# A message-passing layer over a 5000 x 5000 matrix: where each column group's first loads land, when the neighbour counts are spread, and x in two pieces

## The chip, the cores and the metric

The kernel runs on one core of one Trainium2 chip. The metric is the device time of one execution in microseconds (us), lower is better. The kernel before was timed three times: median 266.12 us, from 265.71 to 266.26.

## The reference

`x` is 5000 x 64, `adj` is 5000 x 5000, all in 32-bit floats:

```
h = maximum(layernorm(x), 0)
neighbors = (adj @ h) / (num_neighbors[:, None] + 1e-7)
out = x + relu(concatenate([h, neighbors]) @ fc_w.T + fc_b)
```

Nearly all the data is the matrix: 100 MB of it are read once. `fc_w` is 64 x 128, so its left half works on `h` itself and its right half on the sum over the neighbours.

## The kernel before

The right half of `fc_w` is applied to `h` before the large product (`weigh` on TensorE, copied to `g_sb` by `copy_g` on ScalarE), so that the large product gives the weighted neighbour sums at once. The matrix is handed over transposed, its rows (the inner dimension, 5000) cut into 39 **tiles** of 128 and a rest of 8 rows. Nine blocks of four tiles and one of three make ten **steps** m = 0 to 9.

**Column groups.** The columns (the nodes of the output) are cut into three groups, each stored for itself: group 0 has 2048 columns, group 1 has 2560, group 2 the last 392. TensorE goes through all 39 tiles for group 0, then for group 1, then for group 2. `multiply` (line 544) multiplies one tile for all columns of the group. It issues 8 MATMUL records a tile in group 0, 12 in group 1 and 4 in group 2 (a 32-bit product takes two). The sums stay in the PSUM tiles `acc` (for group 2 it is the tile that is named `turned`). `remainder` (line 555) adds the rest of 8 rows once per group, from `adj_rem`.

**Loads.** SyncE (SP) issues the loads of the matrix one after another into one buffer `raw` of 32768 elements a lane, all on one queue. `STEPS` gives how many tiles one load of each step has, 4, 2 or 1. The loads are numbered through: 0 to 9 are group 0, 10 to 22 group 1, 23 to 36 group 2. A load of four tiles has 4.19 MB in group 0, 5.24 MB in group 1 and 0.80 MB in group 2. `place(n)` says where in `raw` a load lands. Each group uses the buffer as a ring of so many tiles from a start: `RING` holds the start and the length, both in tiles of that group. Group 0 has a ring of 16 tiles from element 0, group 1 of 12 tiles (30720 elements) from element 0, group 2 of 60 tiles from its tile 20 (element 7840).

**What lets a load start.** The last MATMUL of a load counts `load_used` up. `loads_before(n)` finds the last earlier load whose place overlaps that of load n, and SP waits for `load_used` to pass it before it issues load n. SP issues in order, so a load behind a waiting one waits too. TensorE waits for each load's own semaphore before its first tile.

```
return max([k + 1 for k in range(n) if place(k) < place_end(n) and place(n) < place_end(k)] + [n - LANDINGS + 1, 0])
```

**Other work on TensorE.** Tables that are keyed by (group, tile) say after which tile something else is done: `TURN_AFTER` and `WEIGH_AFTER` (transposing `h` and weighing it, set by set, in group 0), `SPREAD_AFTER` (five `spread` calls, lines 523 to 533), `REM_AFTER` (`remainder`) and `FLIP_AFTER` (turning the finished sums back, lines 569 to 571). `spread(b)` turns the reciprocals of the neighbour counts into the layout of the sums; ScalarE copies each result to `rnn_bc` (`copy_spread`, line 309), and `spread(b)` from the third on waits for the copy of the one two before. VectorE multiplies the finished sums with them (`scale`, line 422, behind `wait_sums`) and, after the flip, adds and clips (`finish`).

**The start.** SP first loads `x` (1.18 MB, line 226) and its last nodes, then the matrix. ScalarE issues the weights `w_both` and the bias on its own queue. VectorE and ScalarE normalize `x` in five sets. TensorE can transpose the first set, but waits for `w_both` before it weighs it, and group 0's tile 0 needs that result.

Of the kernel before, what the change touches and what calls it, by code (L numbers as in the profile page):

```python
# [13 lines left out]
BLOCK = 512  # L14
RUN = BLOCK // LANES
# [14 lines left out]
GROUPS = [(0, 4, 0), (4, 5, 2), (9, 1, 5)]  # L30
ALIGN = 1


STEPS = [(4, 4, 4, 4, 4, 4, 4, 4, 4, 4), (4, 4, 4, 4, 4, 4, 4, 4, 2, 1), (4, 4, 4, 4, 4, 4, 4, 2, 2, 1)]
RING = [(0, 16), (0, 12), (20, 60)]


def gnn_layer(nc, x, adj_groups, num_neighbors, fc_t, fc_b, out):
# [23 lines left out]
    BT = 2 * RUN  # L62
    SETS = TILES // BT
    PAIRS = FULL // 2
    ALONE, LAST = PAIRS, PAIRS + 1
    WIDTH = [v.shape[1] for v in adj_groups]
    WIDEST = max(WIDTH) // BLOCK

# [2 lines left out]

    def sides(g, b):

        w = BLOCK if b < ALONE else BLOCK // 2 if b == ALONE else SIDE
        c = (b - GROUPS[g][2]) * 2 * BLOCK
        return [(0, c, w), (1, c + w, w)]


# [7 lines left out]
    def place(n):  # L86

        g, m, i0, _ = LOADS[n]
        return (RING[g][0] + (m * RUN + i0) % RING[g][1]) * WIDTH[g]

    def place_end(n):
        return place(n) + (LOADS[n][3] - LOADS[n][2]) * WIDTH[LOADS[n][0]]

    def loads_before(n):

        return max([k + 1 for k in range(n) if place(k) < place_end(n) and place(n) < place_end(k)] + [n - LANDINGS + 1, 0])

    assert max(place_end(n) for n in range(len(LOADS))) <= RAW


    TURN_AFTER = {(0, 3): 1, (0, 7): 2, (0, 13): 3, (0, 21): 4}
    WEIGH_AFTER = {(0, 5): 1, (0, 11): 2, (0, 19): 3, (0, 27): 4}
    SPREAD_AFTER = {(0, 31 + b): b for b in range(SETS)}
    REM_AFTER = {(0, 37): 0, (1, 11): 1, (2, 3): 2}
    FLIP_AFTER = {(1, 7): 0, (1, 9): 1, (2, 9): 2, (2, 13): 3, (2, 17): 4}
    PRELOAD_AFTER = (2, 25)
    LN_OPS = 8
# [1 line left out]
    with ExitStack() as ctx:  # L109
# [105 lines left out]
        @block.sync  # L215
        def _(sp):
            def load(n):
                g, m, i0, i1 = LOADS[n]
                w = WIDTH[g]
                if loads_before(n):  # L220
                    sp.wait_ge(load_used, loads_before(n))
                r = RUN if m < FULL else TAIL_RUN
                rows = adj_groups[g][m * BLOCK:m * BLOCK + r * LANES, 0:w].rearrange("(p i) c -> p (i c)", i=r)
                sp.dma_start(raw[:, place(n):place_end(n)], rows[:, i0 * w:i1 * w]).then_inc(loaded(n)[0], 16)

            sp.dma_start(flat(x_sb[:, 0:ROWS, :]), x[0:TAIL0, :].rearrange("(p r) f -> p (r f)", r=ROWS)
                         ).then_inc(x_loaded[0], 16)
            sp.wait_ge(x_cleared, 1)
            sp.dma_start(tail(x_sb), tail_nodes(x)).then_inc(x_loaded[1], 16)
            for n in range(len(LOADS)):  # L230
                load(n)
            sp.wait_ge(out_ready, LAST + 1)
            sp.dma_start(tail_nodes(out), tail(out_sb)).then_inc(last_stored, 16)
            sp.wait_ge(last_stored, 16)
# [11 lines left out]
        def _(act):  # L246
# [58 lines left out]

            def copy_spread(b):
                act.wait_ge(spread_done, b + 1)
                w = BLOCK if b < PAIRS else BLOCK // 2 + SIDE
                nc.scalar.activation(rnn_bc[:, b, 0:w], y[b % 2][:, 0:w], ACT.Copy).then_inc(spread_copied, 1)  # L309

            def store(g):
# [29 lines left out]
        def _(dve):  # L341
# [13 lines left out]

            def normalize(b):
                base = LN_OPS * b
                dve.wait_ge(x_loaded[0], 16)
                if b == SETS - 1:
                    dve.wait_ge(x_loaded[1], 16)  # L360
                for rows, narrow, wide in parts(b):
# [50 lines left out]

            def wait_sums(g, b):
                dve.wait_ge(load_used, (FIRST_LOAD + [len(LOADS)])[g + 1])
                dve.wait_ge(spread_copied, min(b, SETS - 1) + 1)

            def scale(g, b):

# [15 lines left out]

            def scale_last(g):
                wait_sums(g, LAST)
                dve.wait_ge(flipped, PAIRS)
                for i in range(2):
                    nc.vector.tensor_tensor(sums[0][:, i * LAST_LANES:(i + 1) * LAST_LANES],
                                            tile_major(acc[LAST][:, 0:SIDE], 2)[:, i, :],  # L440
                                            rnn_bc[:, ALONE, BLOCK // 2 + i * LAST_LANES:BLOCK // 2 + (i + 1) * LAST_LANES],
                                            ALU.mult).then_inc(scaled, 1)

            def finish(b):
                m0, m1 = 2 * b, min(2 * b + 2, FULL)
                o, to_add = blocks(out_sb, m0, m1), blocks(x_sb, m0, m1)
                dve.wait_ge(flipped, b + 1)
                nc.vector.tensor_tensor(o, split(y[b % 2][:, 0:RUN * F * (m1 - m0)]), o, ALU.add).then_inc(summed, 1)  # L448
                dve.wait_ge(summed, b + 1)
                nc.vector.scalar_tensor_tensor(o, o, 0.0, to_add, ALU.max, ALU.add).then_inc(out_ready, 1)  # L450
# [19 lines left out]
            add_bias(3)  # L470
            prepare_halves()
            add_bias(4)
            for b in banks(0):
                scale(0, b)
            for b in banks(0):
                finish(b)
            scale(1, 2)
            scale(1, 3)
            scale_alone(1)
            for b in banks(1):  # L480
                finish(b)
            scale_last(2)
            finish_last()

        @block.tensor
        def _(pe):
# [27 lines left out]
            def spread(b):  # L514
# [2 lines left out]
                    pe.wait_ge(self_copied, 2 * SETS)  # L517
                else:
                    pe.wait_ge(spread_copied, b - 1)
                if b < PAIRS:  # L520
                    for i in range(RUN):
                        t = i * FULL + 2 * b
                        last = nc.tensor.matmul(y[b % 2][:, i * LANES:(i + 1) * LANES], flat(rnn_wide[:, t:t + 2, :]),  # L523
                                                ident[:], start=True, stop=True)
                else:
                    for s in range(2):
                        k = slice(s * HALF, (s + 1) * HALF)
                        for i in range(RUN):
                            last = nc.tensor.matmul(y[b % 2][k, i * HALF:(i + 1) * HALF], rnn_wide[:, i * FULL + FULL - 1, :],  # L529
                                                    ident[:, k], start=True, stop=True, tile_position=(0, s * HALF))  # L530
                        for i in range(2):
                            c = BLOCK // 2 + i * LAST_LANES
                            last = nc.tensor.matmul(y[b % 2][k, c:c + LAST_LANES], rnn_wide[:, ROWS + 2 * s + i, :],
                                                    ident[:, 0:LAST_LANES], start=True, stop=True,
                                                    tile_position=(0, s * HALF))
# [24 lines left out]
            def flip(b):  # L560
# [4 lines left out]
                    pe.wait_ge(out_ready, b - 1)  # L565
                for i in range(RUN):
                    c = slice(i * LANES, (i + 1) * LANES)
                    if b < PAIRS:
                        last = nc.tensor.transpose(y[b % 2][:, c], sums[b % 2][:, c], ident[:])  # L569
                    else:  # L570
                        last = nc.tensor.matmul(y[b % 2][:, i * F:(i + 1) * F], cen[:, c], ident_twice[:],  # L571
# [20 lines left out]
            for n in range(len(LOADS)):  # L592
                g, m, i0, i1 = LOADS[n]
                pe.wait_ge(*loaded(n))
                for i in range(i0, i1):
# [5 lines left out]
                        turn(TURN_AFTER[at])  # L601
                    if at in WEIGH_AFTER:
                        weigh(WEIGH_AFTER[at])
                    if at in SPREAD_AFTER:
                        if SPREAD_AFTER[at] == 0:
                            pe.wait_ge(rnn_chain, 3)
                        spread(SPREAD_AFTER[at])
                    if at in REM_AFTER:
                        remainder(REM_AFTER[at])
                    if at in FLIP_AFTER:  # L610
# [31 lines left out]
```

## Time and profile before

| | us |
|---|---|
| median of three runs | 266.12 |
| lowest and highest | 265.71, 266.26 |
| the profiled execution, own time | 265.64 |
| its span | 263.9 |
| TensorE matmuls busy | 203.5 (77%) |
| VectorE busy | 35.9 |
| ScalarE busy | 15.2 |

The profile is of one execution. Its span runs from the first to the last record; its own time is 1.74 us longer. The queue of SP moved 101.22 of the 102.84 MB; the mean over the span is 390 GB/s. The chain of waits that ended last lies 51% on transfers and 47% on TensorE. In a view of windows, "DMA share" is the mean busy share of the 16 DMA engines; a short window can show over 1, since a transfer's packets are counted where they are recorded. "PEclk" is the clock that TensorE was granted, 1.00 for 2.4 GHz and 0.50 for 1.2 GHz.

### The profile page before, as it was taken

To read this page: it belongs to the slowest core of one execution; us is meant where nothing else is said; L and a number is where in the kernel's file an instruction comes from. 1 tells how busy PE (TensorE), PEld (TensorE's weight loads), DVE (VectorE), ACT (ScalarE), POOL (GpSimd) and SP (SyncE) were. 2 spreads that over 40 slices of the span, in tenths; PEclk is the share of its full clock that TensorE was granted. 3 is DMA by queue.
4 is the path that set the end of the run, shared out by engine and by line. 5 is a ranking of instruction groups with operands and counts; after the bars stand their busy time and mean duration, and the time that the engine had idled before them with its cause. 6 is when DMAs were issued, how large, how long until landed. Compare 5 with 4: busy or idle time off the path is not lost.

```text
span 263.9 us, 2548 instructions
## 1 busy us (share of the span) xinstructions
PE 203.5 (77%) x1156; PEld 89.2 (34%) x1156; DVE 35.9 (14%) x80; ACT 15.2 (6%) x35; POOL 3.0 (1%) x8
## 2 busy tenths in 40 slices
PE   0102899999999979950199959786969859999995
PEld 0102334343334425620033324232323313344784
DVE  0730036333500100010000022000000000000521
ACT  2210011120010001100000000000000000000000
POOL 4000000000000000000000000000000000000000
PEclk9999999999999999995569999997979997999999
DMA  7999999999999994039999999999999999999992
GB/s 279 400 441 385 438 417 441 428 422 446 407 442 427 435 416 205 2 112 422 460 410 447 447 397 456 435 420 410 456 440 428 405 430 419 427 421 421 418 398 79
DMA packets 7848, 102.84 MB, mean 390 GB/s; under 512 B 1478, under 2 KB 3286, under 8 KB 4766
## 3 DMA queue, kind: packets, MB, share of 16 engines
q1 hardware_dynamic: 5892, 101.22, 90.4%
q10 hardware_dynamic: 1946, 1.46, 1.7%
q8 instruction: 9, 0.15, 0.2%
q14 instruction: 1, 0.01, 0.0%
HBM read 101.40 MB, written 1.28 MB: 389 GB/s over the span
## 4 chain that ended last, share of the span: by engine, by line
DMA 51%; PE 47%; ACT 1%; DVE 0%; issue 0%; SPq 0%
DMA raw<-adj_group 42%; PE acc L544 36%; DMA w_both<-fc_t 9%; PE turned L544 5%; PE y L506 2%; PE y L523 1%; PE turned L493 1%; PE acc L555 1%; PE y L569 0%; PE y L571 0%; ACT L318 0%; PE y L529 0%; ACT g_sb L303 0%; PE y L579 0%; DVE out_sb L456 0%
## 5 line engine op out<-in xcount | busy, mean ns | idle before, releaser
L544 PE MATMUL acc<-raw,g_sb 128*64 128x512 f32 (+1 forms) x780 | 166.1, 579 | 33.5 <-DMA raw<-adj_group 32.5
L544 PEld LDWEIGHTS acc<-raw,g_sb 128*64 128x64 f32 x780 | 58.1, 143 | 130.6 <-issue 86.7
L422 DVE TENSOR_TENSOR sums<-acc,rnn_bc 128x512 f32<-128x512 f32 x4 | 2.6, 686 | 109.8 <-PE acc L544 109.8
L506 PE MATMUL y<-w_both,ht 64*128 64x128 f32 (+1 forms) x80 | 7.6, 317 | 12.4 <-DMA w_both<-fc_t 12.4
L544 PE MATMUL turned<-raw,g_sb 128*64 128x196 f32 x156 | 14.2, 332 | 0.0
L493 PE MATMUL turned<-ident,h_pairs 128*128 128x128 f32 x20 | 3.7, 315 | 11.5 <-DVE h_pairs L385 11.5
L506 PEld LDWEIGHTS y<-w_both,ht 64*128 64x128 f32 x80 | 6.2, 215 | 16.1 <-DMA w_both<-fc_t 12.8
L544 PEld LDWEIGHTS turned<-raw,g_sb 128*64 128x64 f32 x156 | 10.8, 137 | 2.2 <-issue 0.3
L448 DVE TENSOR_TENSOR out_sb<-y,out_sb 128x512 f32<-128x512 f32 (+1 forms) x5 | 3.2, 638 | 45.5 <-PE y L569 44.4
L394 DVE TENSOR_TENSOR out_sb<-y,bias 128x256 f32<-128x256 f32 x10 | 3.8, 420 | 39.8 <-ACT g_sb L303 20.7
L493 PEld LDWEIGHTS turned<-ident,h_pairs 128*128 128x128 f32 x20 | 2.4, 156 | 14.7 <-issue 13.1
L303 ACT ACTIVATE g_sb<-y 128x256 f32<-128x256 f32 x10 | 3.3, 381 | 40.2 <-PE y L506 28.3
L523 PEld LDWEIGHTS y<-ident,rnn_wide 128*128 128x128 f32 x32 | 3.9, 191 | 3.2 <-issue 3.2
L523 PE MATMUL y<-ident,rnn_wide 128*128 128x128 f32 x32 | 4.6, 288 | 0.0
L373 DVE TENSOR_REDUCE var<-sums 128x8 f32<-128x512 f32 x5 | 3.4, 686 | 8.6 <-ACT sums L277 8.6
L555 PE MATMUL acc<-adj_rem,g_sb 128*64 128x512 f32 (+1 forms) x20 | 4.5, 549 | 0.0
L362 DVE TENSOR_REDUCE mean<-x_sb 128x8 f32<-128x512 f32 (+1 forms) x6 | 3.5, 590 | 5.1 <-DMA x_sb<-x 5.1
L297 ACT ACTIVATE ht<-turned 128x512 f32<-128x512 f32 x5 | 3.0, 597 | 19.0 <-PE turned L493 19.0
L309 ACT ACTIVATE rnn_bc<-y 128x512 f32<-128x512 f32 (+1 forms) x5 | 2.9, 587 | 19.1 <-PE y L523 16.5
L369 DVE TENSOR_TENSOR cen<-x_sb,mean 128x512 f32<-128x512 f32 (+1 forms) x6 | 3.5, 602 | 0.2
L277 ACT ACTIVATE sums<-cen 128x512 f32<-128x512 f32 x5 | 3.1, 625 | 7.2 <-DVE cen L369 5.9
L381 DVE TENSOR_TENSOR cen<-cen,rstd 128x512 f32<-128x512 f32 x5 | 3.5, 691 | 0.2
(48 smaller groups left out, 38.6 us busy)
## 6 DMA issues: line engine op xcount, KB each, us to landing
raw<-adj_group SPq DMA_DIRECT2D x8, 5120.0 KB, 27.6
raw<-adj_group SPq DMA_DIRECT2D x9, 4096.0 KB, 25.2
raw<-adj_group SPq DMA_DIRECT2D x7, 784.0 KB, 19.5
raw<-adj_group SPq DMA_DIRECT2D x2, 2560.0 KB, 23.3
raw<-adj_group SPq DMA_DIRECT2D x3, 1280.0 KB, 21.5
raw<-adj_group SPq DMA_DIRECT2D x1, 3072.0 KB, 26.8
raw<-adj_group SPq DMA_DIRECT2D x4, 392.0 KB, 20.5
x_sb<-x SPq DMA_DIRECT2D x1, 1152.0 KB, 5.7
```

What stands on the lines that cost most here:

```text
L303: nc.scalar.activation(g_sb[:, t0:t0 + RUN, :], split(y[s][:])[:, :, F:2 * F], ACT.Copy).then_inc(g_copied, 1)
L362: last = nc.vector.tensor_reduce(narrow(mean[:]), rows, AX_X, ALU.add)
L369: last = nc.vector.tensor_tensor(wide(cen[:]), rows, m.unsqueeze(len(m.shape)).to_broadcast(list(rows.shape)), ALU.subtract)
L373: nc.vector.tensor_reduce(var[:], sums[0][:].rearrange("p (t f) -> p t f", f=F), AX_X, ALU.add).then_inc(ln_dve, 1)
L381: nc.vector.tensor_tensor(c, c, bcast(rstd[:]), ALU.mult).then_inc(ln_dve, 1)
L394: nc.vector.tensor_tensor(to, split(y[s][:])[:, :, 0:F], bias[:].unsqueeze(1).to_broadcast([LANES, RUN, F]), ALU.add).then_inc(self_copied, 1)
L448: nc.vector.tensor_tensor(o, split(y[b % 2][:, 0:RUN * F * (m1 - m0)]), o, ALU.add).then_inc(summed, 1)
L493: last = nc.tensor.transpose(turned[:, c], h_pairs[b % 2][:, c], ident[:])
L506: last = nc.tensor.matmul(y[s][:, c:c + (F if apart else 2 * F)], ht[b % 2][k, c:c + LANES], w_both[k, 0:F if apart else 2 * F], start=Tru ...
L523: last = nc.tensor.matmul(y[b % 2][:, i * LANES:(i + 1) * LANES], flat(rnn_wide[:, t:t + 2, :]), ident[:], start=True, stop=True)
L544: last = nc.tensor.matmul(acc[b][s * HALF:(s + 1) * HALF, 0:width], g_sb[:, t, :], raw[:, c + c0:c + c0 + width], start=t == 0, stop=t == ...
L555: last = nc.tensor.matmul(acc[b][s * HALF:(s + 1) * HALF, 0:width], g_sb[:, CH, :], adj_rem[:, c0 // BLOCK, c:c + width], start=False, sto ...
```

## The change

Four things change.

1. **Where loads land.** `RING` now holds the length and an offset, and a load's place is the tile number plus the offset, modulo the length. Group 0 keeps its 16 tiles from element 0. Group 1 keeps its ring of 12 tiles, but its tile 0 lands at place 6 (element 15360). Group 2 has a ring of 83 tiles (32536 elements) whose tile 0 lands at place 59 (element 23128).
2. **The sizes of group 1's loads.** So that no load wraps around the end of the ring, steps 1, 4 and 7 of group 1 come in two loads of 2 tiles and not in one of 4. The loads are now 0 to 9, 10 to 25 and 26 to 39.
3. **The order on TensorE.** All five `spread` calls come after the last tile of group 0, where they stood after tiles 31 to 35. The remainder of group 0 comes after tile 33, where it came after tile 37. `wait_sums` now waits for all five copies.
4. **x** comes in two transfers of 18 rows a lane each, 0.59 MB, that count the same semaphore.

`BANK_BLOCKS` writes out which column blocks a PSUM bank holds, (0, 2, 4, 6, 8, 9); it gives the same blocks as 2 b did, and `ALONE` is 4 as before.

```diff
+BANK_BLOCKS = (0, 2, 4, 6, 8, 9)
-STEPS = [(4, 4, 4, 4, 4, 4, 4, 4, 4, 4), (4, 4, 4, 4, 4, 4, 4, 4, 2, 1), (4, 4, 4, 4, 4, 4, 4, 2, 2, 1)]
-RING = [(0, 16), (0, 12), (20, 60)]
+STEPS = [(4, 4, 4, 4, 4, 4, 4, 4, 4, 4), (4, 2, 4, 4, 2, 4, 4, 2, 2, 1), (4, 4, 4, 4, 4, 4, 4, 2, 2, 1)]
+RING = [(16, 0), (12, 6), (83, 59)]
...
-        return (RING[g][0] + (m * RUN + i0) % RING[g][1]) * WIDTH[g]
+        return (RING[g][1] + m * RUN + i0) % RING[g][0] * WIDTH[g]
...
-        return max([k + 1 for k in range(n) if place(k) < place_end(n) and place(n) < place_end(k)] + [n - LANDINGS + 1, 0])
+        over = [k + 1 for k in range(n) if place(k) < place_end(n) and place(n) < place_end(k)]
+        return max(over + [n - LANDINGS + 1, 0])
...
-    SPREAD_AFTER = {(0, 31 + b): b for b in range(SETS)}
-    REM_AFTER = {(0, 37): 0, (1, 11): 1, (2, 3): 2}
+    SPREAD_AFTER = (0, 38)
+    REM_AFTER = {(0, 33): 0, (1, 11): 1, (2, 3): 2}
...
-            sp.dma_start(flat(x_sb[:, 0:ROWS, :]), x[0:TAIL0, :].rearrange("(p r) f -> p (r f)", r=ROWS)
-                         ).then_inc(x_loaded[0], 16)
+            for k in range(2):
+                r = slice(ROWS // 2 * k, ROWS // 2 * (k + 1))
+                sp.dma_start(x_sb[:, r, :], x[0:TAIL0, :].rearrange("(p r) f -> p r f", r=ROWS)[:, r, :]
+                             ).then_inc(x_loaded[0], 16)
...
-                dve.wait_ge(x_loaded[0], 16)
+                dve.wait_ge(x_loaded[0], 32)
...
-                dve.wait_ge(spread_copied, min(b, SETS - 1) + 1)
+                dve.wait_ge(spread_copied, SETS)
...
-                    if at in SPREAD_AFTER:
-                        if SPREAD_AFTER[at] == 0:
-                            pe.wait_ge(rnn_chain, 3)
-                        spread(SPREAD_AFTER[at])
+                    if at == SPREAD_AFTER:
+                        pe.wait_ge(rnn_chain, 3)
+                        for b in range(SETS):
+                            spread(b)
```

How the instructions move. First TensorE from the fourth spread of before up to the first tile of group 1, in the kernel before (L523, L529 and L533 are spreads, L544 the tiles, L555 the remainder; 64x256 is a form that only group 1 has, so the row with x8 ahead of it is the last tile of group 0 and four of group 1):

```order
L523 MATMUL y<-ident,rnn_wide 128x128 x4
L544 MATMUL acc<-raw,g_sb 64x512 x4
L529 MATMUL y<-ident,rnn_wide 64x64 x4
L533 MATMUL y<-ident,rnn_wide 64x98 x2
L529 MATMUL y<-ident,rnn_wide 64x64 x4
L533 MATMUL y<-ident,rnn_wide 64x98 x2
L544 MATMUL acc<-raw,g_sb 64x512 x8
L555 MATMUL acc<-adj_rem,g_sb 64x512 x4
L544 MATMUL acc<-raw,g_sb 64x512 x8
L544 MATMUL acc<-raw,g_sb 64x256 x2
```

The same place in the changed kernel, from tile 28 of group 0 on (lines 529 to 539 are the spreads there, 550 the tiles, 561 the remainder):

```order
L550 MATMUL acc<-raw,g_sb 64x512 x24
L561 MATMUL acc<-adj_rem,g_sb 64x512 x4
L550 MATMUL acc<-raw,g_sb 64x512 x20
L529 MATMUL y<-ident,rnn_wide 128x128 x16
L535 MATMUL y<-ident,rnn_wide 64x64 x4
L539 MATMUL y<-ident,rnn_wide 64x98 x2
L535 MATMUL y<-ident,rnn_wide 64x64 x4
L539 MATMUL y<-ident,rnn_wide 64x98 x2
L550 MATMUL acc<-raw,g_sb 64x512 x4
L550 MATMUL acc<-raw,g_sb 64x256 x2
```

The remainder moved ahead by four tiles, and nothing but tiles stands between it and group 0's end; all five spreads stand between group 0's last tile and group 1's first.

Second, SP's loads from group 0's first to group 1's second size, before:

```order
L224 DMA raw<-adj_group 128x8192 x9
L224 DMA raw<-adj_group 128x6144
L224 DMA raw<-adj_group 128x10240 x8
L224 DMA raw<-adj_group 128x5120 x2
L224 DMA raw<-adj_group 128x2560 x3
L224 DMA raw<-adj_group 128x1568 x7
```

And in the changed kernel, from the two pieces of x on:

```order
L232 DMA x_sb<-x 128x1152 x2
L235 DMA x_sb<-x 98x2x128
L228 DMA raw<-adj_group 128x8192 x9
L228 DMA raw<-adj_group 128x6144
L228 DMA raw<-adj_group 128x10240
L228 DMA raw<-adj_group 128x5120 x2
L228 DMA raw<-adj_group 128x10240 x2
L228 DMA raw<-adj_group 128x5120 x2
L228 DMA raw<-adj_group 128x10240 x2
L228 DMA raw<-adj_group 128x5120 x4
L228 DMA raw<-adj_group 128x2560 x3
```

Group 1 now begins with a load of 4 tiles (128x10240) and two of 2 tiles (128x5120), where it began with eight of 4 tiles; x has one row more ahead of everything.

## Rows read from the trace of the kernel before

**Rows 1.** The page: the span in 40 equal slices, 6.6 us each.

```profile
span 263.9 us, 2548 instructions
...
PEclk9999999999999999995569999997979997999999
DMA  7999999999999994039999999999999999999992
GB/s 279 400 441 385 438 417 441 428 422 446 407 442 427 435 416 205 2 112 422 460 410 447 447 397 456 435 420 410 456 440 428 405 430 419 427 421 421 418 398 79
```

**Rows 2.** The chain that ended last: start us, us, what.

```profile
1.67 23.28 DMA w_both<-fc_t
...
68.62 28.33 DMA raw<-adj_group
...
116.02 0.33 SPq L224
...
116.39 26.59 DMA raw<-adj_group
```

**Rows 3.** Windows: start and end, length, busy us, PEclk, DMA share, GB/s.

```profile
95.00:99.00 4.00, 2.47 (x14) 0.89 (x13) 0.00 (x0) 0.60 (x1) 0.00 (x0) 1.00 0.96 414
102.00:103.00 1.00, 1.00 (x10) 0.88 (x12) 0.00 (x0) 0.00 (x0) 0.00 (x0) 1.00 0.23 98
106.00:116.00 10.00, 9.99 (x64) 5.78 (x63) 0.00 (x0) 1.12 (x2) 0.00 (x0) 1.00 0.02 4
120.00:122.00 2.00, 0.00 (x0) 0.00 (x0) 0.00 (x0) 0.00 (x0) 0.00 (x0) 0.50 0.76 328
191.00:203.50 12.50, 10.39 (x51) 3.86 (x48) 0.00 (x0) 0.00 (x0) 0.00 (x0) 0.86 1.00 431
222.00:236.00 14.00, 14.00 (x80) 5.53 (x78) 0.00 (x0) 0.00 (x0) 0.00 (x0) 1.00 1.00 424
239.50:258.30 18.80, 18.80 (x184) 13.43 (x182) 5.66 (x10) 0.00 (x0) 0.00 (x0) 1.00 1.01 404
```

**Rows 4.** Timeline of PE: start us, us, instructions [idle before <-releaser].

```profile
25.00 2.08 PE L506 MATMUL y<-w_both,ht 64*128 64x128 f32 x16 [12.42 <-DMA w_both<-fc_t]
...
87.29 7.09 PE L544 MATMUL acc<-raw,g_sb 128*64 128x512 f32 x32 [0.33 <-DMA raw<-adj_group]
94.31 1.16 PE L523 MATMUL y<-ident,rnn_wide 128*128 128x128 f32 x8
...
112.11 2.16 PE L555 MATMUL acc<-adj_rem,g_sb 128*64 128x512 f32 x8
...
130.90 11.63 PE L544 MATMUL acc<-raw,g_sb 128*64 128x512 f32 x48 [14.91 <-DMA raw<-adj_group]
...
168.24 8.81 PE L544 MATMUL acc<-raw,g_sb 128*64 128x512 f32 x48 [1.39 <-DMA raw<-adj_group]
180.71 10.51 PE L544 MATMUL acc<-raw,g_sb 128*64 128x512 f32 x48 [3.66 <-DMA raw<-adj_group]
193.32 10.51 PE L544 MATMUL acc<-raw,g_sb 128*64 128x512 f32 x48 [2.11 <-DMA raw<-adj_group]
205.78 8.81 PE L544 MATMUL acc<-raw,g_sb 128*64 128x512 f32 x48 [1.95 <-DMA raw<-adj_group]
218.03 25.55 PE L544 MATMUL acc<-raw,g_sb 128*64 128x512 f32 x132 [3.43 <-DMA raw<-adj_group]
...
255.73 4.53 PE L544 MATMUL turned<-raw,g_sb 128*64 128x196 f32 x52
```

**Rows 5.** SP's first load of group 1: its issue, and us from issue to landing.

```profile
L224 SPq DMA_DIRECT2D raw<-adj_group x1: 327/327/327, 116.0 to 116.0; - x1
...
DMA to landing us min/median/max: 14.8/14.8/14.8
```

**Rows 6.** SP's last two loads: their issues, and us to landing.

```profile
L224 SPq DMA_DIRECT2D raw<-adj_group x2: 1612/1616/1620, 243.4 to 245.1; - x2
...
DMA to landing us min/median/max: 14.3/14.7/15.0
```

More of the change, by code:

```diff
@@ L64, in gnn_layer @@
     PAIRS = FULL // 2
-    ALONE, LAST = PAIRS, PAIRS + 1
+    LAST = PAIRS + 1
+    ALONE = [n - m for m, n in zip(BANK_BLOCKS, BANK_BLOCKS[1:])].index(1)
     WIDTH = [v.shape[1] for v in adj_groups]
@@ L72, in sides @@
     def sides(g, b):
-        w = BLOCK if b < ALONE else BLOCK // 2 if b == ALONE else SIDE
-        c = (b - GROUPS[g][2]) * 2 * BLOCK
+        w = SIDE if b == LAST else BLOCK // 2 if b == ALONE else BLOCK
+        c = (BANK_BLOCKS[b] - GROUPS[g][0]) * BLOCK
         return [(0, c, w), (1, c + w, w)]
@@ L307, in copy_spread @@
                 act.wait_ge(spread_done, b + 1)
-                w = BLOCK if b < PAIRS else BLOCK // 2 + SIDE
+                w = BLOCK if b != ALONE else BLOCK // 2 + SIDE
                 nc.scalar.activation(rnn_bc[:, b, 0:w], y[b % 2][:, 0:w], ACT.Copy).then_inc(spread_copied, 1)
@@ L436, in scale_last @@
                 wait_sums(g, LAST)
-                dve.wait_ge(flipped, PAIRS)
+                dve.wait_ge(flipped, LAST)
                 for i in range(2):
@@ L444, in finish @@
             def finish(b):
-                m0, m1 = 2 * b, min(2 * b + 2, FULL)
+                m0, m1 = BANK_BLOCKS[b], BANK_BLOCKS[b + 1]
                 o, to_add = blocks(out_sb, m0, m1), blocks(x_sb, m0, m1)
@@ L472, in _ @@
             add_bias(4)
[L473 to L482, printed above, removed]
+            for g in range(G - 1):
+                for b in banks(g):
+                    if b == ALONE:
+                        scale_alone(g)
+                    else:
+                        scale(g, b)
+                for b in banks(g):
+                    finish(b)
+            scale_last(G - 1)
             finish_last()
@@ L519, in spread @@
                     pe.wait_ge(spread_copied, b - 1)
-                if b < PAIRS:
+                m = BANK_BLOCKS[b]
+                if b != ALONE:
                     for i in range(RUN):
-                        t = i * FULL + 2 * b
+                        t = i * FULL + m
                         last = nc.tensor.matmul(y[b % 2][:, i * LANES:(i + 1) * LANES], flat(rnn_wide[:, t:t + 2, :]),
@@ L528, in spread @@
                         for i in range(RUN):
-                            last = nc.tensor.matmul(y[b % 2][k, i * HALF:(i + 1) * HALF], rnn_wide[:, i * FULL + FULL - 1, :],
+                            last = nc.tensor.matmul(y[b % 2][k, i * HALF:(i + 1) * HALF], rnn_wide[:, i * FULL + m, :],
                                                     ident[:, k], start=True, stop=True, tile_position=(0, s * HALF))
@@ L567, in flip @@
                     c = slice(i * LANES, (i + 1) * LANES)
-                    if b < PAIRS:
+                    if b != ALONE:
                         last = nc.tensor.transpose(y[b % 2][:, c], sums[b % 2][:, c], ident[:])
```

## The prediction

> **What bounds the kernel now.** I read the page's slices first. The transfers run at 9 tenths and 400 to 450 GB/s nearly throughout, with one hole: three slices with 3 tenths or less and 205, 2 and 112 GB/s, around 100 to 119 us [rows 1]. The chain of waits says which work surrounds it. It goes through a load until 96.95, through TensorE until SP issues at 116.02, and through another load that begins at 116.39 [rows 2]. The windows show the edge: share 0.23 from 102 to 103, 0.02 from 106 to 116, so the data stop at 102.2 [rows 3]. In the timeline of TensorE, group 1's first tile stands at 130.90 behind 14.91 us of idle time, and in all of group 1 TensorE waits 1.4 to 3.7 us before each load [rows 4]. So the kernel is bound by its transfers, at 429 GB/s or so, plus one stretch in which nothing is transferred.
>
> The hole is made by the ring. Load 10 begins at element 0, load 8 lay there and load 9 behind it (elements 8192 to 14336). Load 10 is 10240 elements a lane, so it touches load 9's place and waits for `load_used` 10, the last tile of group 0.
>
> **The hole, the main term.** Load 8 lands at 96.95 [rows 2]. Load 9 is 3.15 MB, 7.3 us at 429 GB/s, so it lands at about 104.3. With a full queue, load 10 (5.24 MB, 12.2 us) would land at 116.5. It landed at 116.0 + 14.8 = 130.9 [rows 4, 5]. That is 14.4 us late.
>
> In the changed kernel load 10 takes elements 15360 to 25600 and load 11 25600 to 30720. The last loads there are 6 and 7, so both wait for `load_used` 8. Load 7 is used up at 94.3, where tile 31's products end [rows 4], so both are issued then, 8 us before the data of load 9 end. I went through the next waits in the same way. Data end times: load 10 at 102.2 + 12.2 = 114.4, 11 at 120.5, 12 at 126.6, 13 at 138.8.
>
> - Load 12 (elements 0 to 5120) waits for load 8. TensorE starts load 8 at 97.0, four tiles at (94.31 - 87.29) / 4 = 1.76 us each, plus the remainder, which has as many records as a tile: 105.8. The queue needs it at 120.5.
> - Load 13 (5120 to 15360) waits for load 9: three tiles more, 111.1, needed at 126.6.
> - Load 14 waits for load 10. TensorE is through with it at 116.9 + 8.8 = 125.7 [8.81 in rows 4], needed at 138.8.
>
> From there each load is again issued about 13 us ahead. The smallest margin is the first, 8 us. The hole goes, and every landing behind it comes 14.4 us earlier: **-14.4**.
>
> **The end.** SP's last load is issued at 245.1 and lands 14.3 us later (the later of the two has the shorter time, since they land in order), at 259.4 [rows 6]. The last tiles run without a wait in 255.73 to 260.26 [rows 4]. One tile is 4.53 / 13 = 0.35, so 259.4 + 0.35 is the earliest possible end: TensorE lags by 0.5. This lag comes from the 25.55 us for 11 tiles from 218.03 on: they end at 243.6, while group 1's last load lands at about 218.0 + 9.17 MB / 424 GB/s = 239.7. With step 7 in two pieces, TensorE can start the second half of that stretch earlier: it begins step 7 after 2.62 MB and not 5.24 MB, so the queue of unfinished tiles is about 2 us shorter. In group 2 TensorE needs less than the transfers (7.8 MB at 404 GB/s is 19.4 us [rows 3]; TensorE takes 16.7, from 243.6 to 260.3), so it catches up. Between 0 and 0.5 is gained; as the lag at the start of group 2 becomes smaller than the 2.7 it catches up there, I take **-0.5**.
>
> **Smaller loads.** Three loads of 5.24 MB become six of 2.62 MB. The full ones run at 431 GB/s, the stretch with 2.62 and 1.31 MB at 424 [rows 3]. For 15.7 MB that is 0.6 us if the size makes the difference, 0 if not: **+0.5**, near the upper end because the 404 GB/s of group 2, with smaller ones still, point the same way. SP's three more issues cost 0.33 us each on an engine that otherwise waits.
>
> By the Trainium skill ("DMA: Bandwidth & Descriptors", Anatomy of one DMA) every transfer pays a fixed cost of about 2.0 us besides its bytes. Paid in full by the three extra loads, that would turn the sum from -14.4 into -8.4. The first load into an empty queue does show such a cost, 14.8 - 12.2 = 2.6 us [rows 5], but TensorE's starts behind a full queue, 205.78 and 218.03, are 12.25 apart, which is 5.24 MB at 428 GB/s with nothing added [rows 4]. So I count it as a rival alone.
>
> **The spreads and the remainder.** Five spreads at 1.16 us [rows 4] move from group 0's tiles to behind them: 111.1 + 5.8 = 116.9, beside load 10's landing at 116.5. The move costs TensorE 0.4 us there, and it then waits for load 13 (landing 140.9, TensorE free at about 134.5) by over 6 us. Cost at the end: 0. If that cover were gone it would be 5.8. What is behind them: load 11's and 12's products start no earlier than they land plus 1 us or so. ScalarE issues group 1's remainder load behind the five copies, at about 118, and it is wanted after tile 11, past 140. VectorE's first `scale` goes from 116.0 to about 118 and is wanted by the flip after tile 7, past 130. The chain of rnn values was ready at 94.31, when the first spread ran. The remainder before load 8's end delays load 12's issue by 1.8, with a margin of 15.
>
> **x in two pieces.** SP issues 0.4 us more ahead of the matrix; the engines are then still busy with x (1.18 MB, 2.8 us). What may change is `w_both`, which took 23.28 us to land beside the large loads [rows 2]. If it lands early, TensorE's first tile moves from behind 25.00, where it weighs the first set, to load 0's landing near 17. That gives nothing at the end: TensorE had caught up with the transfers by 87.29 and 97.0 anyway, where it waits for loads 7 and 8 [rows 4], and no load of group 0 was late. If x's landing costs another 2.6 us [rows 5], the 12.42 us of TensorE's wait for `w_both` cover it [rows 4]. Bounds 0 and 0.4, taken **0**.
>
> **Sum.** -14.4 - 0.5 + 0.5 = -14.4. The profiled execution took 265.64, so 251.2. It lies 0.5 below the median of the three runs, 266.12; I add that: **251.7**.
>
> **The rivals.**
>
> *TensorE's clock costs something at the end.* The idle time before load 13 is about 6 us, and other waits of 2 to 4 us stay. After 14.91 us idle the granted clock was 0.50, that is 1.2 GHz [rows 3], and the burst took 11.63; after 3.66 and 2.11 idle it took 10.51, after 1.95 and 1.39 it took 8.81 [rows 4]. As all are below the 12.2 us of a load, this is hidden in group 1. But if the clock falls in the last 30 us, where the loads are small and the lag counts, 10.51 - 8.81 = 1.7 us or part of it reach the end: 251.7 + 0.5 (the gain at the end lost) + 1.7 = 253.9 at most. For it: the smaller pieces bring TensorE closer to the transfers, so it stops more often. Against: in the stretch from 218.03 it fell before too and TensorE nearly caught up. Chance 0.14. The Trainium skill ("TensorE: Matmul & The Clock Gate", HAM oscillation — how this bites in real kernels) says that a kernel whose bursts alternate with waits for transfers starts every burst throttled. By that rule each load of group 1 would take 10.5, and the sum would be the same; the trace agrees for two of the four bursts named here.
>
> *The hole closes only in part.* If load 10 still waited for load 9, it would be issued at 111.1 and not 116.0, as spreads and remainder no longer stand before it: 4.9 us gained, 261.2. The code speaks against it. The same would come about if TensorE were 8 us later in group 0 than before. Chance 0.04.
>
> *Each extra load pays for itself.* Three times 2.6 us: 251.7 - 0.5 + 7.8 = 259.0. Chance 0.02.
>
> *Slower: TensorE stays at the lower clock in group 1.* Then a load's products take 2 x 8.8 = 17.6 us, TensorE sets the pace in place of the transfers, and eight full loads' worth plus the last add 5.4 us each, over 40 in all: about 300. It decides from the point where the bursts take on average 12.2 + 14.4 / 9 = 13.8 us, so where over half of each is at 1.2 GHz. The worst burst seen is 11.63 after 15 us idle. Chance 0.02.
>
> **How the numbers follow.** Forecast 0.78, the rivals 0.14, 0.04, 0.02 and 0.02. Low end: the sum without the 0.5 for small loads, and against the profiled run, 250.7, less 0.4 for the spread of the runs: 250.3. High end: the clock rival, 253.9 (the forecast without the 0.5 at the end, and 1.7). That leaves out 0.08 and what the forecast's own terms miss. 0.2% is 0.5 us, about what a measurement of this kernel can tell from no change. All cases but the slower one and a residue are faster: faster 0.97, same 0.01, slower 0.02.
>
> **What would show it.** Right: no slice without transfers around 100 to 119; SP's issues of loads 10 and 11 at about 94; group 1's first tile near 117, then a wait of about 6 us before tile 8; spreads in one block at 111; the last load landing near 245. The x step is seen in `w_both`'s landing and the first tile's start, with group 0's end unmoved. Wrong: any slice below 8 tenths in the middle, a last landing later than 246, or TensorE over 1 us behind it.

## The result and the profile after

The changed kernel takes 250.89 us (median of four runs, 250.73 to 252.17) against 266.0 for the kernel before. The ratio is 0.9443, with a 95% interval of 0.941 to 0.9475: 15 us less. The forecast was 251.7 with a range of 250.3 to 253.9. The profiled execution took 250.73, its span is 248.9.

The page first, its slices (6.2 us each now), beside [rows 1]:

```profile
span 248.9 us, 2552 instructions
...
PEclk9999999997999999999999579999769999999999
DMA  9999999999999999999999999999999999999992
GB/s 299 408 376 433 421 425 438 427 427 427 446 432 421 432 424 421 461 428 401 421 464 434 428 417 415 431 450 432 434 432 414 425 427 431 411 418 419 411 390 73
```

The slices of the transfers are all at 9 up to the last. Between the first and the last, the lowest has 376 GB/s; before, three in the middle had 205, 2 and 112. The mean over the span is 413 GB/s and was 390. In the row PEclk, the clock that TensorE was granted fell three times for a while (the 7, the 5 and 7, the 7 and 6).

The chain that ended last, beside [rows 2]:

```profile
1.69 14.84 DMA w_both<-fc_t
...
66.30 30.41 DMA raw<-adj_group
...
110.75 30.12 DMA raw<-adj_group
...
229.11 15.66 DMA raw<-adj_group
```

No step of the chain is a load that waited for the end of group 0 and found an empty queue. The step at 110.75 is load 13, issued some 16 us before the queue came to it. The chain is 68% transfers now, and was 51%.

SP's loads 10 and 11, the place that the prediction rests on, beside [rows 5]:

```profile
L228 SPq DMA_DIRECT2D raw<-adj_group x2: 328/380/432, 94.2 to 94.5; - x2
...
DMA to landing us min/median/max: 22.0/25.0/27.9
```

They were issued at 94.2 and 94.5 and landed 22.0 and 27.9 us later, at 116.2 and 122.4. Load 10 had landed at 130.9.

TensorE's timeline, beside [rows 4]:

```profile
16.58 2.08 PE L511 MATMUL y<-w_both,ht 64*128 64x128 f32 x16 [4.05 <-DMA w_both<-fc_t]
19.51 9.28 PE L550 MATMUL acc<-raw,g_sb 128*64 128x512 f32 x32 [0.85 <-ACT g_sb L309]
...
96.75 3.65 PE L550 MATMUL acc<-raw,g_sb 128*64 128x512 f32 x16 [2.62 <-DMA raw<-adj_group]
...
116.17 17.41 PE L550 MATMUL acc<-raw,g_sb 128*64 128x512 f32 x96 [0.17 <-DMA raw<-adj_group]
...
140.91 7.44 PE L550 MATMUL acc<-raw,g_sb 128*64 128x512 f32 x24 [6.75 <-DMA raw<-adj_group]
...
155.36 17.36 PE L550 MATMUL acc<-raw,g_sb 128*64 128x512 f32 x96
178.44 11.75 PE L550 MATMUL acc<-raw,g_sb 128*64 128x512 f32 x48 [5.72 <-DMA raw<-adj_group]
191.08 17.41 PE L550 MATMUL acc<-raw,g_sb 128*64 128x512 f32 x96 [0.89 <-DMA raw<-adj_group]
...
215.34 8.81 PE L550 MATMUL acc<-raw,g_sb 128*64 128x512 f32 x48 [1.59 <-DMA raw<-adj_group]
...
244.81 0.55 PE L550 MATMUL turned<-raw,g_sb 128*64 128x196 f32 x4 [0.39 <-DMA raw<-adj_group]
```

The first burst of group 1 starts at 116.17 with 0.17 us of idle time, where 14.91 stood. The wait for load 13 is 6.75 us, and after it the burst is slow (24 records in 7.44 us; the next 24, from 148.87 on, took 4.52 at full clock). The last load lands at 229.11 + 15.66 = 244.77 and one tile follows.

Three windows, beside [rows 3]: the middle of the former hole, the small loads of group 1, and group 2.

```profile
106.00:116.00 10.00, 10.00 (x78) 6.34 (x74) 0.00 (x0) 2.39 (x4) 0.00 (x0) 1.00 0.97 416
216.00:224.00 8.00, 8.00 (x46) 3.02 (x42) 0.00 (x0) 0.00 (x0) 0.00 (x0) 1.00 1.00 420
230.00:240.00 10.00, 9.63 (x98) 7.29 (x97) 3.62 (x6) 0.00 (x0) 0.00 (x0) 1.00 1.02 411
```

106 to 116 has 416 GB/s; it had 4.

**Where the 15 us come from.** The landings give the account. Load 10: 130.9 to 116.2, 14.7. From load 10 to the last landing: 128.5 before (130.9 to 259.4), 128.6 now, so the same bytes in three more transfers cost 0.1. From the last landing to TensorE's last tile: 0.9 before (259.4 to 260.3), 0.6 now (244.8 to 245.4). What follows it: 3.6 before, 3.5 now. That is 14.7 - 0.1 + 0.3 + 0.1 = 15.0, the whole difference of the spans.

**What the hole had hidden.** A load counts its semaphore up in 16 steps, and it has landed with the sixteenth. The trace has the time of each step. Behind the hole the 16 steps of load 10 lay within 0.8 us (130.08 to 130.85); in the changed kernel they lie 2.3 us apart (113.87 to 116.13). So the first part of load 10 comes 16.2 us earlier and the last part 14.7. Without a pause in the queue the parts drift on: for the last load the first step comes at 240.5, the eighth at 242.9 and the sixteenth at 244.8. Before, they came at 256.5, 256.8 and 259.4. The last landing, which the whole kernel now waits for, is that of the latest parts alone. No run tries to change this.

### The profile page after: what moved, and what is told of

The parts are those of the page before. It is cut to its first block, busy times and chain, and to the rows that moved or that the text cites. A ratio compares the mean times of both kernels' runs of the same rounds, so it can differ in the third digit from the quotient of the medians.

```text
span 248.9 us, 2552 instructions
## 1 busy us (share of the span) xinstructions
PE 204.0 (82%) x1156; PEld 87.1 (35%) x1156; DVE 35.9 (14%) x80; ACT 15.2 (6%) x35; POOL 3.1 (1%) x8
## 4 chain that ended last, share of the span: by engine, by line
DMA 68%; PE 29%; ACT 1%; DVE 0%; issue 0%; SPq 0%
DMA raw<-adj_group 62%; PE acc L550 25%; DMA w_both<-fc_t 6%; PE acc L561 2%; PE turned L550 1%; PE y L511 1%; ACT L324 0%; SPq L228 0%; ACT g_sb L309 0%; PE y L575 0%; DVE out_sb L462 0%; PE y L591 0%; PE turned L561 0%; DVE sums L445 0%
## 5 line engine op out<-in xcount | busy, mean ns | idle before, releaser
L550 PEld LDWEIGHTS acc<-raw,g_sb 128*64 128x64 f32 x780 | 56.9, 143 | 126.5 <-issue 91.6
L550 PE MATMUL turned<-raw,g_sb 128*64 128x196 f32 x156 | 14.9, 334 | 1.0 <-DMA raw<-adj_group 1.0
L498 PEld LDWEIGHTS turned<-ident,h_pairs 128*128 128x128 f32 x20 | 2.4, 156 | 14.7 <-issue 13.0
L529 PEld LDWEIGHTS y<-ident,rnn_wide 128*128 128x128 f32 x32 | 3.7, 191 | 0.8 <-issue 0.8
L529 PE MATMUL y<-ident,rnn_wide 128*128 128x128 f32 x32 | 3.9, 280 | 0.0
```

Source lines behind the costliest of these rows:

```text
L498: last = nc.tensor.transpose(turned[:, c], h_pairs[b % 2][:, c], ident[:])
L550: last = nc.tensor.matmul(acc[b][s * HALF:(s + 1) * HALF, 0:width], g_sb[:, t, :], raw[:, c + c0:c + c0 + width], start=t == 0, stop=t == ...
```

## The experiments

Each was timed against the kernel before in five rounds, but e11, which is a single execution. My theory was that the place of loads 10 and 11 is everything; the rivals gave parts of the gain to the spreads, to x and to the load sizes.

### e1: the places alone

The kernel before with `RING`, `STEPS` and `place` of the changed one; x in one piece, spreads and remainder where they were. (It also has the rewritten bank tables, and with them a wait of VectorE's last `scale` for one more flip. In the profiles that flip is done 8 us before it is wanted.)

```diff
-STEPS = [..., (4, 4, 4, 4, 4, 4, 4, 4, 2, 1), ...]
-RING = [(0, 16), (0, 12), (20, 60)]
+STEPS = [..., (4, 2, 4, 4, 2, 4, 4, 2, 2, 1), ...]
+RING = [(16, 0), (12, 6), (83, 59)]
```

> The kernel before with the new places and the new load sizes of group 1 alone: x in one piece, the spreads after tiles 31 to 35, the remainder after tile 37. My theory: the place of load 10 is the whole gain, because loads 10 and 11 are issued at about 94 with load 7 used up. Expected 250.9 us (250.6 to 251.3), load 10 landing near 116.3, no slice without transfers. Rival 1: the spreads behind group 0 are needed, since they free loads 8 and 9 some 5 us earlier; then some of the hole comes back, 1 to 5 us, 252 to 256. Rival 2: x in two pieces brings part of the gain, 0.5 to 1 us: 251.4 to 252.

251.17 us (251.01 to 251.26), ratio 0.9446 [0.9431, 0.9461]. That is the ratio of the full change. The places, with the load sizes that go with them, give the whole gain; e6 takes the sizes away again.

### e2: the old places with all the rest

```diff
-RING = [(16, 0), (12, 6), (83, 59)]
+RING = [(16, 0), (12, 0), (83, 20)]
```

> The changed kernel, but group 1 begins at element 0 again (and group 2 at its tile 20, element 7840), with the new sizes, spreads, remainder and x. My theory: load 10 waits for the last tile of group 0, which now ends at 110.7 instead of 116.0; the data stop at 102.2 again, load 10 lands at 110.7 + 14.8 = 125.5 in place of 116.2. Expected 250.9 + 9.3 = 260.2 (259.7 to 260.8). Rival: if the spreads, x or the sizes carry part of the gain, it comes out under 259.5; if the place does nothing, 250.9.

262.02 us (260.96 to 263.88), ratio 0.986 [0.9828, 0.9891]. The place is worth 11 us in this company, and the hole is back. Group 2's place went back too, but no gain can lie there: from load 10 to the last landing the kernel before took 128.5 us and the changed one 128.6. The time came out nearly 2 us above what I had expected (260.2). The profiled execution took 262.74. Its timeline of TensorE:

```profile
97.04 5.35 PE L550 MATMUL acc<-raw,g_sb 128*64 128x512 f32 x16 [2.65 <-DMA raw<-adj_group]
...
112.62 3.90 PE L529 MATMUL y<-ident,rnn_wide 128*128 128x128 f32 x32
...
128.79 19.17 PE L550 MATMUL acc<-raw,g_sb 128*64 128x512 f32 x96 [10.80 <-DMA raw<-adj_group]
```

And its first load of group 1 on SP:

```profile
L228 SPq DMA_DIRECT2D raw<-adj_group x1: 327/327/327, 112.7 to 112.7; - x1
...
DMA to landing us min/median/max: 16.0/16.0/16.0
```

Two things differ from my sum. The first 16 records after the wait for load 8 took 5.35 us and not 3.65, so the last tile of group 0 ends at 112.6 and not 110.7. And load 10 took 16.0 us from issue to landing, not 14.8. The first looked like the clock; e8, e11 and e10 follow it up. The second is taken up in e9.

### e3: x in one piece

The changed kernel with the single transfer of x from the kernel before.

```diff
-            for k in range(2):
-                r = slice(ROWS // 2 * k, ROWS // 2 * (k + 1))
...
+            sp.dma_start(flat(x_sb[:, 0:ROWS, :]), x[0:TAIL0, :].rearrange("(p r) f -> p (r f)", r=ROWS)
```

> The changed kernel with x in one transfer. My theory: w_both lands near 25 again and not at 16.5, TensorE starts 8 us later and has caught up by load 8; the time stays 250.9 (within 0.3). Rival: the early start matters, through the margin of the issue of load 4 or through fewer small packets beside large ones; then 251.4 to 252.

251.22 us (250.82 to 252.29), ratio 0.9455 [0.9436, 0.9474]. The timeline of TensorE:

```profile
24.68 2.08 PE L509 MATMUL y<-w_both,ht 64*128 64x128 f32 x16 [12.38 <-DMA w_both<-fc_t]
...
97.14 3.65 PE L548 MATMUL acc<-raw,g_sb 128*64 128x512 f32 x16 [2.63 <-DMA raw<-adj_group]
```

It weighs the first set at 24.68 and not at 16.58, 8 us later, and waits for load 8 all the same, 2.63 us here and 2.62 in the changed kernel. The early start is lost in the waits of group 0. The median is 0.3 above that of the changed kernel, at the edge of what I had given, and the intervals overlap.

### e4: the spreads between the tiles

The changed kernel with `SPREAD_AFTER` and `REM_AFTER` of before.

```diff
-    SPREAD_AFTER = (0, 38)
-    REM_AFTER = {(0, 33): 0, (1, 11): 1, (2, 3): 2}
+    SPREAD_AFTER = {(0, 31 + b): b for b in range(SETS)}
+    REM_AFTER = {(0, 37): 0, (1, 11): 1, (2, 3): 2}
```

> The changed kernel with the five spreads after tiles 31 to 35 and the remainder after tile 37 again. My theory: group 0's last tile ends 5 us later, load 13 is issued at about 116 where the queue needs it at 126.6; TensorE is free for load 10 at about the same time as before. 250.9 (within 0.3). Rival: the later issue of loads 12 and 13 lets the queue run low and costs 0.5 to 5 us.

251.49 us (250.93 to 252.75), ratio 0.947 [0.9445, 0.9494]. Two of its five executions are near 252.7. The median is 0.6 above that of the changed kernel, outside the 0.3 that I had given and inside the rival's range. But its interval overlaps that of the changed kernel, and e1, with the same order and x in one piece, took 251.17. So with the new places the order is worth some tenths of a us at most, and these runs cannot tell that from nothing.

### e5: group 1 in loads of two tiles

```diff
-STEPS = [..., (4, 2, 4, 4, 2, 4, 4, 2, 2, 1), ...]
+STEPS = [..., (2, 2, 2, 2, 2, 2, 2, 2, 2, 1), ...]
```

> The changed kernel with steps 0 to 8 of group 1 all in loads of 2 tiles: 21 loads of group 1 in place of 16, the same places and bytes. My theory: a transfer behind a full queue costs only its bytes, at 424 GB/s and not 431 at most, so 26 MB at the lower rate give 0 to 1 us: 250.9 to 251.9. Rival: the fixed 2.6 us of a first transfer is paid by each of the 5 more: 263.9.

251.59 us (251.02 to 252.0), ratio 0.9453 [0.9428, 0.9478]. Five transfers more cost 0.7 us by the medians and 0.3 by the ratios, less than these runs can tell from nothing. In the profile the last load lands at 245.32, 128.8 us after group 1's first four tiles (128.6 in the changed kernel). The rival with 2.6 us for each is out by 12 us. The fixed cost of a transfer is hidden behind a full queue.

### e6: group 1 in loads of four tiles

The other way to the same end: all loads of steps 0 to 7 have four tiles again, group 1 begins at place 8, so that load 10 lies on load 7's place, and load 11 waits for load 9.

```diff
-STEPS = [..., (4, 2, 4, 4, 2, 4, 4, 2, 2, 1), ...]
-RING = [(16, 0), (12, 6), (83, 59)]
+STEPS = [..., (4, 4, 4, 4, 4, 4, 4, 4, 2, 1), ...]
+RING = [(16, 0), (12, 8), (83, 0)]
```

> The changed kernel with the old sizes of group 1, loads of 4 tiles in steps 0 to 7, its tile 0 at place 8 of the 12 (element 20480), and group 2 from element 0. Load 10 waits for load 7 as in the changed kernel, load 11 for load 9: issued at 110.7, where the queue needs it at about 114.4. My theory: no transfer is missing, TensorE's lag at the end is about 0.8 in place of 0.6 and the rate of 5.24 MB loads gives 0 to 0.5 back: 250.9 (250.4 to 251.3). Rival: load 11 comes too late by the latency of a transfer, and 1 to 3 us of the hole return: 252 to 254.

251.22 us (250.84 to 251.58), ratio 0.9439 [0.9415, 0.9464], the same as the changed kernel. In the profile, the slices of the transfers and TensorE's first burst after the wait for load 8, the wait for load 11, and the last stretch of group 1:

```profile
DMA  8999999999999999999999999999999999999991
```

```profile
96.92 5.35 PE L550 MATMUL acc<-raw,g_sb 128*64 128x512 f32 x16 [2.63 <-DMA raw<-adj_group]
...
129.40 10.17 PE L550 MATMUL acc<-raw,g_sb 128*64 128x512 f32 x48 [2.94 <-DMA raw<-adj_group]
...
203.98 25.46 PE L550 MATMUL acc<-raw,g_sb 128*64 128x512 f32 x132 [3.37 <-DMA raw<-adj_group]
```

The clock had fallen here too (5.35 us), so load 11 was issued only at about 112.6, some 2 us before the queue needed it. That was a little late. Load 10 landed at 116.3 and load 11 at 129.4, 13.1 us later, where the next one took 12.1. So 0.9 us of the hole is back in this execution, the low end of the rival's 1 to 3. The last stretch, 132 records in 25.46 us, is what it was in the kernel before (25.55). TensorE ends 1.6 us after the last landing (244.5 to 246.1), and not 0.6. Neither shows in the median: the five executions are 250.84, 250.94, 251.22, 251.50 and 251.58, and the profile is of the one at 251.50. What the split of step 7 gives is not more than the scatter.

### e7: x in two pieces on the kernel before

```diff
+            for k in range(2):
+                r = slice(ROWS // 2 * k, ROWS // 2 * (k + 1))
```

> The kernel before with x in two pieces alone. My theory: w_both lands some 8 us earlier, TensorE starts earlier and waits more in group 0, load 8 still lands at 97, the hole stays: 265.9 (265.5 to 266.5), and if TensorE's clock falls between loads 8 and 9, up to 1.7 us more, since here the hole ends when TensorE does. Rival: the early start shortens the hole, 265 or less.

266.04 us (265.55 to 267.74, 12 runs), ratio 1.0006 [0.9988, 1.0024]. TensorE's timeline:

```profile
13.93 2.08 PE L508 MATMUL y<-w_both,ht 64*128 64x128 f32 x16 [1.44 <-DMA w_both<-fc_t]
...
97.60 1.94 PE L546 MATMUL acc<-raw,g_sb 128*64 128x512 f32 x8 [1.53 <-DMA raw<-adj_group]
...
131.60 10.60 PE L546 MATMUL acc<-raw,g_sb 128*64 128x512 f32 x48 [15.01 <-DMA raw<-adj_group]
```

TensorE weighs the first set 11 us earlier than in [rows 4], and waits for load 8 by 1.53 us, as the kernel before did:

```profile
97.00 1.94 PE L544 MATMUL acc<-raw,g_sb 128*64 128x512 f32 x8 [1.53 <-DMA raw<-adj_group]
```

The hole stays, 15.01 us of idle time.

### e8: spreads behind group 0 on the kernel before

```diff
-    SPREAD_AFTER = {(0, 31 + b): b for b in range(SETS)}
-    REM_AFTER = {(0, 37): 0, (1, 11): 1, (2, 3): 2}
+    SPREAD_AFTER = (0, 38)
+    REM_AFTER = {(0, 33): 0, (1, 11): 1, (2, 3): 2}
```

> The kernel before with the five spreads behind group 0 and the remainder after tile 33 alone, old places, old sizes, x whole. My theory: load 10 is issued with the last tile's end at about 111 and not 116.0, so the hole shortens by 4.9 to 5.3 us: 261.0, or up to 262.7 where TensorE's clock falls at load 8 as in the run with old places. Rival: load 10 does not follow the last tile, 265.9.

262.45 us (260.38 to 262.69), ratio 0.9849 [0.9818, 0.988]. One execution took 260.38, the other five 262.21 to 262.69. The profile is of the one at 260.38:

```profile
96.61 3.65 PE L544 MATMUL acc<-raw,g_sb 128*64 128x512 f32 x16 [2.61 <-DMA raw<-adj_group]
...
110.50 3.90 PE L523 MATMUL y<-ident,rnn_wide 128*128 128x128 f32 x32
...
126.93 11.60 PE L544 MATMUL acc<-raw,g_sb 128*64 128x512 f32 x48 [11.06 <-DMA raw<-adj_group]
```

With the old places the order is worth 3.5 us: load 10 follows group 0's last tile, and that tile ends at 110.5 instead of 116.0. In this kernel TensorE does set the end of a transfer's wait, and there a fast TensorE counts. The change as a whole has two cures for the same 14.4 us; the places take all of it, so the order has nothing left to give.

### e11: the kernel of e8 once more

> The kernel of e8 once more, for its profile. Theory: if this execution takes about 262.5, its profile shows tiles 32 and 33 in 5.3 us and not 3.65, with a granted clock under 1.00 between 95 and 104, and load 10 issued near 112.4. Rival: a time of 262.5 with 3.65 us for the two tiles.

This execution took 262.11. TensorE's timeline and the window of the clock:

```profile
96.58 5.35 PE L544 MATMUL acc<-raw,g_sb 128*64 128x512 f32 x16 [2.62 <-DMA raw<-adj_group]
...
112.16 3.90 PE L523 MATMUL y<-ident,rnn_wide 128*128 128x128 f32 x32
...
128.45 11.64 PE L544 MATMUL acc<-raw,g_sb 128*64 128x512 f32 x48 [10.93 <-DMA raw<-adj_group]
```

```profile
95.00:100.00 5.00, 3.42 (x8) 0.99 (x10) 0.00 (x0) 0.00 (x0) 0.00 (x0) 0.66 0.97 418
```

5.35 us for the 16 records and not 3.65, PEclk 0.66 in the window (the same window of e8's profile, at 260.38, has 1.00), the last tile's end 1.66 us later, load 10's landing 1.52 later, the time 1.73 longer. The two levels of this kernel are the two outcomes of one wait: after 2.6 us idle TensorE is at 1.2 GHz for a while, or it is not. Both outcomes have been seen in a profile, with the time that goes with each.

### e10: two spreads in the wait for load 8

```diff
-    SPREAD_AFTER = (0, 38)
+    SPREAD_AFTER = {(0, 31): (0, 1), (0, 38): (2, 3, 4)}
...
-                        for b in range(SETS):
+                        for b in SPREAD_AFTER[at]:
```

> As the run e8, but the first two spreads stand after tile 31, in the wait for load 8, and only three behind group 0. Theory: the five slow executions of e8 (262.2 to 262.7 against 260.4) are those in which TensorE's clock fell in its 2.6 us wait for load 8; with the wait filled to 0.4 us the clock holds, and all executions are near 260.4 (within 0.5). Rival: the scatter has another cause, and the median stays at 262.4.

261.23 us (260.72 to 261.52), ratio 0.9827 [0.9813, 0.984]. TensorE's timeline:

```profile
94.18 2.05 PE L523 MATMUL y<-ident,rnn_wide 128*128 128x128 f32 x16
96.87 3.65 PE L544 MATMUL acc<-raw,g_sb 128*64 128x512 f32 x16 [0.64 <-DMA raw<-adj_group]
...
110.75 2.05 PE L523 MATMUL y<-ident,rnn_wide 128*128 128x128 f32 x16
...
127.12 10.37 PE L544 MATMUL acc<-raw,g_sb 128*64 128x512 f32 x48 [12.85 <-DMA raw<-adj_group]
```

The wait is 0.64 us, the burst after it 3.65. All five executions lie within 0.8 us, and none at 262.2 or above. The upper level is gone, as expected. The median is 0.8 above 260.4, at the edge of what I had given or past it, and I do not know from what.

### e9: why load 10 took 16 us and not 14.8

```diff
+            load_rem(1)
             for b in range(SETS):
                 copy_spread(b)
-            load_rem(1)
```

> The kernel before with spreads behind group 0 and the remainder after tile 33 (as in the run e8), and ScalarE issuing group 1's remainder load ahead of the five copies and not behind them. In the two runs with a hole and the spreads behind it, load 10 took 16.0 and 16.3 us from issue to landing, in the two with the spreads before it 14.8 and 14.9. Theory: the 40 short packets of the remainder load run beside load 10 there and make it late; issued early they are gone, and load 10 takes 14.8: 1.4 us less than e8, 261.0 (259.0 where TensorE's clock holds). Rival: the difference has another cause, 262.4 as e8.

261.53 us (260.36 to 262.63), ratio 0.9838 [0.9807, 0.9868]: three executions at 260.4 to 260.6 and three at 262.4 to 262.6, the two levels of e8. The profiled one took 262.43:

```profile
96.94 5.35 PE L544 MATMUL acc<-raw,g_sb 128*64 128x512 f32 x16 [2.63 <-DMA raw<-adj_group]
...
128.87 11.69 PE L544 MATMUL acc<-raw,g_sb 128*64 128x512 f32 x48 [10.99 <-DMA raw<-adj_group]
```

SP issued load 10 at 112.63, so it took 16.2 us though the remainder load had been issued at 104.0. My theory falls. What the profiles still show is a packet of another queue. The queues in the window 116 to 132 of the kernel before, and then of e8:

```profile
q1 hardware_dynamic: 175, 6.51, 99.0%
q10 hardware_dynamic: 36, 0.06, 1.0%
```

```profile
q1 hardware_dynamic: 177, 6.59, 95.5%
q10 hardware_dynamic: 48, 0.08, 1.3%
q8 instruction: 1, 0.02, 0.4%
```

In all of the kernels with 16 us (e2, e8, e9, e10, e11) an instruction packet of 0.02 MB (queue q8) ran beside load 10; in the two with 14.8 and 14.9 (the kernel before and e7) there was none beside it. The semaphore steps of load 10 say more. In all seven profiles the first 15 of the 16 steps come 13.9 to 15.0 us after the issue. The sixteenth comes at 14.8 and 14.9 in the two, and at 16.0 to 16.3 in the five. So it is one part in sixteen that is late, and not the load as a whole. The instruction packet took 0.88 to 0.97 us there, which fits a delay of one part by one packet. But the trace does not tell which DMA engine a packet ran on, and no run moves the packet, so this cause is not shown.

The same is seen elsewhere, and it explains why e8 is 5.3 us shorter although its load 10 landed only 4.0 us earlier (126.9 against 130.9). In the kernel before, the next such packet ran at 160.0, beside load 13, and there the sixteenth step came 0.9 us behind the fifteenth. These rows are of the kernel before, the bursts behind loads 12 and 13:

```profile
155.15 4.52 PE L544 MATMUL acc<-raw,g_sb 128*64 128x512 f32 x24 [2.72 <-DMA raw<-adj_group]
...
168.24 8.81 PE L544 MATMUL acc<-raw,g_sb 128*64 128x512 f32 x48 [1.39 <-DMA raw<-adj_group]
```

They are 13.1 us apart, and in e8 12.2 (151.16 and 163.35). From load 13 on e8 is 4.9 us ahead. The last 0.3 is TensorE's lag at the end.

## Why the prediction was right

**The bound.** Read as transfers plus one hole, from the slices, the chain and the windows. This held: the kernel now has no hole and is bound by its transfers throughout.

**The hole, -14.4.** It measured 14.7. Loads 10 and 11 were issued at 94.2, load 10 landed at 116.2 (forecast 94.3 and 116.5). The margins were as worked out: load 12 was issued at 105.6 (105.8), load 13 at 110.7 (111.1), and load 13 landed at 140.9 (140.9). The run with the places alone shows it to be the whole effect, and the run with the old places shows the hole to come back.

**The end, -0.5.** It measured -0.3, and the reason I gave for it, the split of step 7, is not shown. e8 has no split and the same lag as the changed kernel: its last stretch, 132 records, took 23.85 us at full clock, and TensorE ended 0.6 us after the last landing. Where the clock had fallen in that stretch and there was no split, it took 25.55 and 25.46 us, and the lag was 0.9 (the kernel before) and 1.6 (e6). So the clock in that stretch changes the lag; what the split adds is open.

**Smaller loads, +0.5.** It measured +0.1 in the landings. This term was mis-sized: I read the difference between 431 and 424 GB/s as the price of the size, and the run with loads of two tiles throughout allows 0.2 us in the landings for five more transfers (0.3 to 0.7 in the times). The 404 GB/s of group 2, which pulled me to the upper end, says nothing about 20 KB packets, since its own are 6 KB and less.

**The fixed cost per transfer.** The Trainium skill ("DMA: Bandwidth & Descriptors", Anatomy of one DMA — SWDGE (gpsimd) path) gives about 2.0 us for a transfer that GpSimd issues; the prediction took it for SyncE's loads as well. Paid by each of the three extra loads it would make the forecast an estimated 257.7 (the rival's 2.6 us made 259.0). Both the changed kernel and the run with loads of two tiles show it hidden behind the full queue.

**Spreads and x, 0 each.** Both right, for the reasons given: the cover was there in the trace (a wait of 6.75 us before load 13; waits for loads 7 and 8). One reading was off: before load 11 TensorE waited 0.50 us, and not 1.4 to 3.7 as before the later loads of group 1. Nothing in the sum hangs on it. That the order is worth 3.5 us where the hole remains was in the second rival, as the 4.9 us that a partly closed hole would gain; at full clock it came out at 5.3 (260.38 against 265.64), in the median smaller.

**From the profiled run to the median, +0.5.** The changed kernel's profiled run lies 0.2 below its median, so this term was 0.3 too large. The 0.8 us between 251.7 and 250.89 are then 0.3 from the hole, 0.4 from the smaller loads and 0.3 from here, less 0.2 that the end gave less than forecast.

**The rivals.** The clock did fall, in group 0 and for the bursts after the waits of 6.75 and 5.72, and it cost nothing at the end, since none lay in the last 30 us. Its price of 1.7 us per fall holds behind the wait of 2.6 us (5.35 against 3.65). Behind the two long waits of the changed kernel the burst took 2.9 us more (7.44 against 4.52, and 11.75 against 8.81). And I looked for the place where it counts only at the end of the kernel. It counts in the partly closed hole, where group 0's last tile releases a load: e8 is 1.7 us longer with it. The 4.9 us that I gave for that rival left this out. Some executions of the changed kernel and its relatives take 1 to 1.5 us more than the rest (252.17 here, 252.29 with x whole, 252.62 and 252.75 with the spreads between the tiles). No profile is of such an execution, so what they lose is open.

## What to carry to other kernels

Where one buffer is used as a ring by stages with different row widths, write out for each load at a stage's border which earlier load lies under it. If the first load of a stage lies on the last one of the stage before, the queue runs dry for the rest of that stage's work plus the latency of a transfer; an offset in the ring removed it here and cost nothing that the landings show. Issue the first loads well ahead: in e6, with only 2 us of margin, 0.9 us of the hole came back. Then look for the second cure that the change brings along: with the queue kept full, an earlier start and another order on TensorE were worth nothing that these runs can tell (e1, e3, e4), and only the kernel with the hole shows what they give (e7 nothing, e8 3.5 us).

## What the runs showed of the hardware

After a wait of 2.6 us TensorE's clock fell in some executions of one kernel and not in others. Where the burst after the wait is on the path (e8, e9), the times have two levels some 2 us apart (260.4 to 260.6 and 262.1 to 262.7), of which the burst makes 1.7. Two profiles of the same program show both: a wait of 2.62 us with a fallen clock behind it (e11), and one of 2.61 with the full clock (e8). Nor does the length of the wait alone decide it elsewhere: in the kernel before, the burst after 2.72 us of waiting ran at full clock (24 records in 4.52), and the one after 2.11 us did not (48 in 10.51). The Trainium skill ("TensorE: Matmul & The Clock Gate", HAM oscillation — how this bites in real kernels) describes a kernel with longer waits for transfers, in which every burst starts throttled; here, after 2.6 us, 5.35 and 3.65 us both occur.

A first load into an empty queue took 14.8 and 14.9 us in two profiles and 16.0 to 16.3 in five, for the same 5.24 MB. The difference is one of the load's 16 parts, which came over 1 us behind the other 15. It did not depend on the short packets of the remainder load (e9).
